# A two-layer transformer chain on eight cores: layer norm finished tile by tile instead of in groups of four, and fewer projection matmuls per step in the last head pair

## What is computed

```python
def attn(x):                       # 16 heads of 64
    q, k, v = x @ Wq.T + bq, x @ Wk.T + bk, x @ Wv.T + bv
    a = softmax(q k^T / 8) * head_mask
    return (a v) @ Wo.T + bo       # attention b: the same without biases and mask
def ffn(x):                        # linear layer plus 8 rank-16 experts, top 2 of 8 by a router
    return x @ base_w.T + base_b + 2 * sum_e w[e] * (x @ A[e]) @ B[e]
x = x + attn_a(layernorm(x))
x = x + ffn(layernorm(x))
x = x + attn_b(layernorm(x))
x = x + ffn(layernorm(x))
```

## Time and profile before

| | us |
|---|---|
| median of 2 runs (4726.45 to 4733.66) | 4730.05 |
| the profiled execution | 4732.18 |
| its span on the slowest core (core 3) | 4730.8 |
| spans of the eight cores | 4714.9 to 4730.8 |
| TensorE / VectorE / ScalarE / GpSimd busy in the span | 3658.4 / 1790.5 / 2438.7 / 68.9 |
| exponentials of the attention (L578, two groups of 1024) | 1141.0 + 1140.1 |
| mean granted TensorE clock, core by core | 0.917 to 0.924 of full |

### The profile page before, as it was taken

How to read it: one execution, slowest core, us unless ns; L and a number is a source line. 1 busy time by engine, 2 the same in 40 slices (tenths; PEclk the granted TensorE clock), 3 DMA queues, 4 the chain that set the end, 5 groups by cost and what they waited for, 6 DMA issues and landing times.

```text
span 4730.8 us, 60192 instructions; the slowest of 8 cores (4714.9 to 4730.8 us)
## 1 busy us (share of the span) xinstructions
PE 3658.4 (77%) x18800; PEld 1363.1 (29%) x18800; DVE 1790.5 (38%) x4025; ACT 2438.7 (52%) x2433; POOL 68.9 (1%) x134
## 2 busy tenths in 40 slices
PE   3788888956688888884658888888566888888758
PEld 1333333212233333321223333332122333333213
DVE  4333333355433333336533222223555222222463
ACT  0477777700047777760004777776000587787400
POOL 0000000000000000000000000000000000000000
PEclk8999999967899999996779999999678999999878
DMA  4000000010100000010230000001001000000101
GB/s 104 11 16 17 12 12 5 13 20 1 32 10 16 17 12 12 5 28 5 72 102 10 16 17 12 12 5 22 10 1 32 14 17 12 16 8 10 27 1 71
DMA packets 33091, 98.81 MB, mean 21 GB/s; under 512 B 5392, under 2 KB 5520, under 8 KB 31248
## 3 DMA queue, kind: packets, MB, share of 16 engines
q0 software_dynamic: 17600, 44.13, 5.8%
q1 hardware_dynamic: 15184, 50.85, 3.2%
HBM read 122.04 MB, written 17.04 MB: 29 GB/s over the span
## 4 chain that ended last, share of the span: by engine, by line
PE 55%; ACT 20%; DVE 9%; issue 8%; DVEq 6%; DMA 2%; ACTq 1%; SPq 0%
ACT s_pbuf L578 19%; PE psC L586 10%; PE psC L593 6%; DVEq L157 6%; PE psA L566 5%; PE psA L795 5%; PE psD L432 4%; PE psE L432 4%; PE psD L360 4%; PE psB L566 4%; PE psE L360 3%; PE psE L533 2%; PE psD L533 2%; PE psE L468 2%; DVE s_xnT L365 2%
## 5 line engine op out<-in xcount | busy, mean ns | idle before, releaser
L578 ACT ACTIVATE s_pbuf<-psA,s_negbb 128x1024 bf16<-128x1024 f32 x1024 | 1141.0, 1114 | 603.8 <-PE psA L572 507.4
L578 ACT ACTIVATE s_pbuf<-psB,s_negbb 128x1024 bf16<-128x1024 f32 x1024 | 1140.1, 1113 | 219.3 <-PE psB L572 190.9
L586 PE MATMUL psC<-s_pbuf,s_vaug 128*128 128x512 bf16 x2048 | 784.9, 383 | 392.1 <-ACT s_pbuf L578 343.3
L593 PE MATMUL psC<-s_pbuf,s_vaug 128*128 128x512 bf16 x2048 | 781.2, 381 | 4.8 <-DVE s_sumsT L616 4.7
L360 PE MATMUL psD<-s_bigi,s_xns 128*128 128x512 bf16 x512 | 175.9, 478 | 408.2 <-DVE s_xns L351 408.2
L586 PEld LDWEIGHTS psC<-s_pbuf,s_vaug 128*128 128x128 bf16 x2048 | 196.0, 96 | 935.0 <-issue 935.0
L342 ACT ACTIVATE s_lnv<-s_mv,s_epsb 128x4 f32<-128x4 f32 x32 | 9.4, 294 | 805.9 <-DVE s_mv L338 805.9
L572 PE MATMUL psA<-s_qt,s_kt 64*128 64x512 bf16 x1024 | 399.9, 391 | 0.0
L566 PE MATMUL psA<-s_qt,s_kt 64*128 64x512 bf16 x1024 | 399.9, 390 | 0.0
L572 PE MATMUL psB<-s_qt,s_kt 64*128 64x512 bf16 x1024 | 399.7, 390 | 0.0
L566 PE MATMUL psB<-s_qt,s_kt 64*128 64x512 bf16 x1024 | 399.7, 390 | 0.0
(11 more groups left out here) (124 smaller groups left out, 3797.6 us busy)
## 6 DMA issues: line engine op xcount, KB each, us to landing
s_xbuf<-x SPq DMA_DIRECT2D x32, 512.0 KB, 18.1
s_rexp<-hbm_rr SPq DMA_DIRECT2D x64, 256.0 KB, 3.5
y<-s_xbuf SPq DMA_DIRECT2D x32, 512.0 KB, 2.7
s_wpool<-base POOLq DMA_DIRECT2D x8, 1024.0 KB, 11.3
s_wpool<-wo_a POOLq DMA_DIRECT2D x2, 2048.0 KB, 18.0
s_wpool<-wq_a POOLq DMA_DIRECT2D x16, 256.0 KB, 3.7
s_wpool<-wk_a POOLq DMA_DIRECT2D x16, 256.0 KB, 3.8
s_wpool<-wv_a POOLq DMA_DIRECT2D x16, 256.0 KB, 3.7
```

The lines of the kernel that those rows point to most:

```text
L578: P.op("scalar", lambda q, ps=ps, kpar=kpar, hg=hg: q.activation(pbuf[:, kpar * 1024:(kpar + 1) * 1024], ps[:, 0:1024], AF.Exp, bias=negbb ...
L586: P.op("tensor", lambda q, kt=kt, kpar=kpar, par=par: q.matmul(psC[0:128, 0:512], vaug[:, par * NT * 192 + kt * 192:par * NT * 192 + kt * ...
L593: P.op("tensor", lambda q, kt=kt, kpar=kpar, par=par: q.matmul(psC[0:128, 512:1024], vaug[:, par * NT * 192 + kt * 192 + 64:par * NT * 192 ...
```

## The change

The group function is split into one for each tile, `ln_tile_rest(tag, t)`, with its own Ln and Exp of one column. In the attention tail and in the feed-forward stage it is called right behind the statistics of its tile; the deferral of the layer norm by one step in the feed-forward stage is gone. And in the last head pair `pump` puts out three fillers in each step instead of four with a three in every fourth.

```diff
+    def ln_tile_rest(tag, t):
+        P.op("scalar", lambda q, t=t: q.activation(lnv[:, t:t + 1], mv[:, 2 * t + 1:2 * t + 2],
+                                                   AF.Ln, bias=epsb[:, 0:1], scale=1.0),
+             reads=[f"mv.{t}", "epsb"], writes=[f"lnv.{t % 4}"], tag=f"{tag}.lnv.{t}")
+        P.op("scalar", lambda q, t=t: q.activation(rstd[:, t:t + 1], lnv[:, t:t + 1],
+                                                   AF.Exp, bias=0.0, scale=-0.5),
+             reads=[f"lnv.{t % 4}"], writes=[f"rstd.{t}"], tag=f"{tag}.rstd.{t}")
...
     def ln_group(tag, g):
-        P.op("scalar", lambda q, g=g: q.activation(lnv[:, 4 * g:4 * g + 4],
...
         for t in range(g * 4, g * 4 + 4):
...
+            ln_tile_rest(tag, t)
@@ emit_scores
-                    pump(3 if kt % 4 == 3 else 4)
+                    pump(3 if (kt % 4 == 3 or hg == 7) else 4)
@@ attention tail
             if hook is not None:
                 hook.tile(t)
                 hook.stats(t)
-                if t % 4 == 3:
-                    hook.group(t // 4)
+                hook.rest(t)
@@ ffn
-            if hook is not None:
-                if g >= 1 and g <= 4:
-                    for t in range((g - 1) * 4, g * 4):
-                        hook.stats(t)
-                if g >= 2:
-                    hook.group(g - 2)
+            if hook is not None and 1 <= g <= 4:
+                for t in range((g - 1) * 4, g * 4):
+                    hook.stats(t)
+                    hook.rest(t)
```

More of the change, by code:

```diff
@@ L339, in ln_tile_stats @@
              reads=["bn6a", "bn6b"], writes=[f"mv.{t}"], tag=f"{tag}.bna.{t}")
-    def ln_group(tag, g):
-        P.op("scalar", lambda q, g=g: q.activation(lnv[:, 4 * g:4 * g + 4],
[L343 to L349, removed]
-        for t in range(g * 4, g * 4 + 4):
[L351 to L367, removed]
@@ new lines, in ln_tile_rest @@
+    def ln_tile_rest(tag, t):
[5 more added lines that the diff above has]
+             reads=[f"lnv.{t % 4}"], writes=[f"rstd.{t}"], tag=f"{tag}.rstd.{t}")
+        P.op("vector", lambda q, t=t: q.tensor_scalar(
+            xns[:, :], x[:, t * 1024:(t + 1) * 1024],
+            mv[:, 2 * t:2 * t + 1], rstd[:, t:t + 1], OP.subtract, OP.mult),
+            reads=[f"x.{t}", f"mv.{t}", f"rstd.{t}"], writes=["xns"],
+            tag=f"{tag}.norm.{t}")
+        for half in range(2):
+            bk = ("psD", "psE")[(t * 2 + half) % 2]
+            for c in range(4):
+                cc = half * 4 + c
+                P.op("tensor", lambda q, cc=cc, c=c, bk=bk: q.matmul(
+                    bank[bk], xns[:, cc * 128:(cc + 1) * 128],
+                    bigi[:, 384 - c * 128:896 - c * 128],
+                    start=(c == 0), stop=(c == 3)),
+                    reads=["xns", "bigi", bk], writes=[bk], tag=f"{tag}.T.{t}.{cc}")
+            P.op("vector", lambda q, t=t, half=half, bk=bk: q.tensor_copy(
+                xnT3[:, 4 * half:4 * half + 4, t * 128:(t + 1) * 128], bank[bk]),
+                reads=[bk], writes=[f"xnT.w{t // 4}"], tag=f"{tag}.Tev.{t}.{half}")
@@ L375, in build_nc, with __init__ @@
     class Hook:
-        def __init__(self, tile=None, stats=None, group=None):
+        def __init__(self, tile=None, stats=None, group=None, rest=None):
             self.tile = tile or (lambda t: None)
@@ L845, in make_last_hook @@
                         stats=lambda t: ln_tile_stats("s1.0.ln", t),
-                        group=lambda g: ln_group("s1.0.ln", g))
+                        rest=lambda t: ln_tile_rest("s1.0.ln", t),
+                        group=lambda g: [ln_tile_rest("s1.0.ln", t) for t in range(g * 4, g * 4 + 4)])
         return Hook(tile=tile)
```

4 lines of the change are left out of this document (3 added, 1 removed).

## The result

The changed kernel is slower. The median of 11 executions is 4989.21 us (4962.76 to 5105.54) against 4733.81 before; the ratio is 1.052, with a 95% interval of 1.0475 to 1.056. In about half of the executions of either kernel a die ran at a lower clock than the other, and the ratios leave the clearly disturbed ones out; with both dies alike the kernel takes about 4964 us (4730 before), and the profiled execution took 4963.43 us.

The account below looks back on a forecast made before the run. Tails and feed-forward layer norms were taken as bound by a chain going to and fro between engines, attention stages by ScalarE and TensorE; 119 + 92 - 14 + 32 = +229 us on 4732.18 gave 4961 us, range 4850 to 5040.

Parts of the forecast that it names:

- A: Four attention tails: each tile becomes one chain between normalisations, with slow transposes; +119 us, ends 0 and +142.
- B: Feed-forward stages: per-tile layer norm costs 7.6 us a tile at the lower clock; +92 us, ends +5 and +100.
- D: Exchange of the reciprocals: next feed-forward weight loads start later and lie over it; +32 us, ends 0 and +60.
- C: Last head pairs: three fillers a step fill TensorE's idleness in the fourth quarter; -14 us, ends 0 and -20.
- everything at the upper level: Attention tails with TensorE at 2.4 GHz throughout: 127.5 and 121 us, no added time.
- the lower level for all: Feed-forward layer norms: TensorE idles 4.0 us between transposes, so all tiles take 1.2 GHz; 7.6 us a tile.
- +5 for that case: Feed-forward stages with the clock at the upper level throughout: 5.9 us a tile, 23.6 a group, +5 us in all.
- +8 a tail: Exchange at each attention tail: slower rexp loads plus lengthened round trips beside the weight loads; +8 us each.
- The first layer norm: Program's first layer norm, 16 tiles from the input: four small ScalarE pairs instead of one, costed at nothing.
- That the clock stays up: Rival for tails and feed-forward stages: more even TensorE work holds the upper clock; 4755 us, chance 0.12.
- That the exchange is starved: Rival at the exchange of the reciprocals: it waits until the weight loads are through; +60, 4989 us, chance 0.13.
- That tiles overlap: Rival in the tails: next tile's projection passes the waiting transposes, saving 184 us; 4571 us, chance 0.03.

Follow-up runs that it names:

- Experiment 3: Kernel before with only the attention tails per tile (Ln and Exp per tile in the grouped layer norms too); ratio 1.0252, +119 us.
- Experiment 5: Changed kernel plus 16 matmuls per tile in the attention tails, into a bank nobody reads there; ratio 1.0224 against the kernel before.
- Experiment 8: Kernel before with only feed-forward stages per tile, plus 16 matmuls ahead of each tile's transposes there, into a bank nobody reads then; ratio 0.9951.
- experiment 4: Kernel before with only the feed-forward stages per tile (Ln and Exp per tile in the grouped tails too); ratio 1.0103, +49 us.
- experiment 2: Kernel before with three fillers a step in the last head pair and the next weights' loads held until the exchange is through; ratio 0.9954.
- experiment 7: Changed kernel with neighbouring tiles' work overlapped in tails and feed-forward stages, three fillers a step, weight loads held back; ratio 0.939 against the kernel before, about 4442 us.
- Experiments 1: Kernel before with three fillers a step in the last head pair and nothing else; ratio 1.0021, about 4745 us.

## Why the prediction was right

4961 us was forecast and 4963.4 measured. The mechanisms of A and B held. Part of the closeness is luck: D was too small by 18 us, B too large by 8 and C too small a gain by 7.

**A, +119 for +119.5.** The mechanism and the price hold. The chain from normalisation to normalisation is there (9.6 to 10.2 us a tile in attention a against 10.0, 9.0 to 9.7 in b against 9.3), with about 4 us of idleness before slow transposes and a projection behind them in which the clock comes up, early in the first tiles and late in the others. Experiment 3 has the whole term in the tails alone. Experiment 5 shows its cause, which the prediction had only argued from two rows: keep TensorE busy, and the tails come back to within 5.3 us of before. Its tails (128.3 and 121.4) and periods (7.93 and 7.61) are the end "everything at the upper level" of the prediction (127.5 and 121, 7.9 and 7.6). The Trainium skill, "TensorE: Matmul & The Clock Gate", section "HAM oscillation — how this bites in real kernels", describes just this: a burst, a wait, and each burst starting slow. By that rule A lay between its middle and its upper end, and the trace agrees, with 1.87 us behind 4.19 us of idleness.

**B, +92 for +83.8.** By stages 32.6, 15.3 and 34.9 against 37, 18 and 37, and 0.9 in the stage without a layer norm. The mechanism is right: 7.58 us a tile where 7.6 was worked out, but some tiles took 7.2 only, so "the lower level for all" and the 1 us a group for slow starts were a little dear. Experiment 8 shows that the clock is nearly all of it: with it held up, the stages are 3 us above before, where the prediction had given +5 for that case. Not seen was that Ln and Exp per tile are a gain wherever the grouping stays. The change itself gets nothing from it, since it leaves no group, but it cost experiment 4 its expectation.

**C, -14 for -20.6.** The right direction, and its end of -20. The prediction read 4 to 5 us of idleness in the fourth quarter and booked 3.5 a pass; the passes gained 5.15 on the mean. The quarters of the first pass took 28.1, 27.6, 28.8 and 25.1 us with the old pumping (in experiment 4, which leaves it alone) and 25.6, 26.9, 27.0 and 24.5 in the changed kernel: the first three gained 5.0 together, and the fourth, for which I had written about 26.5, took in the fillers of the others and did not grow.

**D, +32 for +49.8, the term that was mis-sized.** The step that failed is the price of +8 a tail, made of "some 9 to 10 us for the two `rexp` loads instead of 7, plus each of the four round trips lengthened by a packet or two of the other queue". In the first exchange the two small stores lost 3.3 and 4.7 us and the loads 3.9 and 0.4, 12.3 in all. Each transfer goes out when the one before has landed, and the three that lie beside GpSimd's loads pay 3.3 to 4.7 us each, however little they carry. Most of the delay lies ahead of a transfer's first packet: the first `rexp` load is issued at 958.51, and up to 963.4 all 91 packets on the DMA engines are those of GpSimd's queue; its own then take 1.5 us as before. In the trace of before they started 1.2 us after the issue, in the other three exchanges of the changed kernel 3.8 to 4.3 us after it. The third transfer lands just behind the end of the loads, so the wait goes with how long the loads take, and the price of +8 left that out. That GpSimd's loads cause it is shown by experiment 2. By the turn-taking rule of the Trainium skill, "DMA: Bandwidth & Descriptors", section "Queues, rings and completion order", the exchange would take at most about twice the wait of 9.7. The trace does not bear this out as a bound: 20.66 is 2.1 times, a store grew fivefold, and the second load by a ninth.

**The first layer norm,** costed at nothing, became shorter: from its first to its last normalisation it takes 105.9 us instead of 108.8, since the step from group to group takes 18.4 us instead of 19.3 to 19.7. In the table these 3 us are in "all the rest".

**The rivals.** That the clock stays up (4755 us) fell with the first tile: 1.87 us. That the exchange is starved (D = +60) was nearer to the measured +49.8 than my own value, and its mechanism is half of what happened: the two stores got through while the loads ran, the first `rexp` load only when they ended. Its 4989 us lie within the stated range too, so the time alone does not decide between it and the forecast; the chain does. That tiles overlap (4571 us) did not happen, because the lists are kept, L536 behind L357; experiment 7, whose code makes that overlap, gets 149 us from the tails, against the 184 that VectorE's bare work had promised, and another 117 from the feed-forward stages.

**The three parts do not add.** Experiments 1, 3 and 4 give 13, 120 and 49 us by their spans, 182 where the change costs 231. Of the missing 49, 22 are the gain of experiment 4 in its grouped tails, which is lost where the tails run tile by tile; some 15 are the exchange (82.6 against 67.2 us of waiting), beside longer loads. The remaining dozen is not placed: the feed-forward stages cost 84 us in the full change against 73 in experiment 4, but experiment 3 has 11 us of the kind in its own 120.

## What to carry to other kernels

Before work on several tiles is cut into a chain per tile, write down what each engine has to do while the chain is at another engine: here TensorE had nothing for some 4 us in every tile and started each burst slow, so the price was in the matmuls, not only in the wait. In this kernel the finer grain paid together with an order that puts the next tile's work into the gap (experiment 7, 0.939, against 1.052 for the same grain without it). A wait released earlier lets loads start earlier or later as well: look what small transfers, one behind the other, they will then lie beside, and hold them back if nobody needs them yet.
